# First attention: the product of probabilities and tokens in three fp32r passes instead of one fp32 pass

## The reference, cut to what matters

```python
kv = jnp.concatenate([memory, layer_input], axis=1)      # 64 + 64 = 128 tokens per sequence
q = (layer_input @ Wq).reshape(b, q_len, n_head, d_head) # 16 heads of 64
k = (kv @ Wk).reshape(b, kl, n_head, d_head)
v = (kv @ Wv).reshape(b, kl, n_head, d_head)
ac = jnp.einsum('bqhd,bkhd->bhqk', q + content_bias, k)
bd = rel_shift(jnp.einsum('bqhd,khd->bhqk', q + position_bias, r))
attn = jax.nn.softmax((ac + bd) / np.sqrt(d_head), axis=-1)  # masked before
ctx = jnp.einsum('bhqk,bkhd->bqhd', attn, v).reshape(b, q_len, n_head * d_head)
out = layer_norm(layer_input + ctx @ Wo, ln1_g, ln1_b)
```

## Time and profile before

| | us |
|---|---|
| median of 3 runs (1932.42, 1933.55, 5223.76) | 1933.55 |
| the profiled execution | 1940.73 |
| its span | 1939.2 |
| PE busy | 1621.0 (84%) |
| DVE busy | 1329.5 (69%) |
| ACT busy | 1199.0 (62%) |
| POOL busy | 946.9 (49%) |

### The profile page before, as it was taken

The page is one execution under the profiler, slowest core; times in us unless marked ns, Lnnn a source line. Parts: engine busy times, 40 slices in busy tenths (PEclk is TensorE's granted clock), DMA queues, the critical chain, the costliest instruction groups (busy, mean ns, idle before and its releaser), DMA issues. The chain is left out here.

```text
span 1939.2 us, 54781 instructions
## 1 busy us (share of the span) xinstructions
PE 1621.0 (84%) x17114; PEld 1295.5 (67%) x17114; DVE 1329.5 (69%) x4084; ACT 1199.0 (62%) x3451; POOL 946.9 (49%) x1389
## 2 busy tenths in 40 slices
PE   6999999999996869999999775479998884448981
PEld 5888888888884747667777662157776664437771
DVE  3777777777775638888777536668887883337772
ACT  2776777677674426677777335468888771137771
POOL 3354344444441454556665434534454444646773
PEclk8999999999998979999999787579999995559996
DMA  9676666766662022221000000000000000136765
GB/s 240 150 155 139 157 148 137 162 141 151 149 146 58 1 92 107 94 105 43 19 18 11 1 1 1 0 4 1 0 10 13 12 9 23 44 110 213 215 212 155
DMA packets 214819, 167.06 MB, mean 86 GB/s; under 512 B 27632, under 2 KB 188784, under 8 KB 214448
## 3 DMA queue, kind: packets, MB, share of 16 engines
q1 hardware_dynamic: 206128, 142.75, 29.1%
q0 software_dynamic: 8576, 22.88, 3.6%
HBM read 91.79 MB, written 73.76 MB: 85 GB/s over the span
## 5 line engine op out<-in xcount | busy, mean ns | idle before, releaser
L738 ACT ACTIVATE sb_probs<-sb_probs,sb_work 128x128 f32<-128x128 f32 x512 | 198.6, 406 | 120.3 <-DVE sb_work L641 120.3
L281 POOL TENSOR_SCALAR sb_next_var_eps<-sb_next_moments 128x1 f32<-128x1 f32 (+1 forms) x184 | 45.3, 246 | 433.2 <-DVE sb_next_moments L721 246.6
L890 POOL TENSOR_TENSOR sb_work<-sb_work,sb_cols 128x512 f32<-128x512 f32 x128 | 134.2, 1048 | 215.6 <-ACT sb_work L1107 133.6
L1033 DVE TENSOR_REDUCE sb_work<-PS 128x8 f32<-128x512 f32 x256 | 175.3, 685 | 46.9 <-PE PS L932 44.5
L1035 DVE TENSOR_TENSOR sb_work<-PS,sb_work 128x512 f32<-128x512 f32 x256 | 177.1, 692 | 8.8
L1067 ACT ACTIVATE sb_work<-sb_work 128x512 f32<-128x512 f32 x256 | 161.6, 631 | 33.4 <-DVE sb_work L1035 27.5
L906 PE MATMUL PS<-sb_ident,sb_work 128*128 128x128 f32 x1024 | 150.0, 287 | 15.9 <-ACT sb_work L1107 10.6
L959 PEld LDWEIGHTS PS<-sb_v_ones,sb_work 128*64 128x64 f32 x4096 | 133.0, 140 | 24.7 <-issue 16.9
L959 PE MATMUL PS<-sb_v_ones,sb_work 128*64 128x18 f32 x4096 | 144.9, 214 | 4.6 <-ACT sb_work L1073 2.8
L1073 ACT ACTIVATE sb_work<-PS 128x512 f32<-128x512 f32 x256 | 139.7, 594 | 10.1 <-PE PS L906 6.8
L906 PEld LDWEIGHTS PS<-sb_ident,sb_work 128*128 128x128 f32 x1024 | 113.8, 145 | 43.5 <-issue 31.3
(11 more groups left out here) (281 smaller groups left out, 4467.1 us busy)
## 6 DMA issues: line engine op xcount, KB each, us to landing
rel_scratch<-sb_work SPq DMA_DIRECT2D x64, 516.0 KB, 7.3
sb_work<-rel_scratch SPq DMA_DIRECT2D x64, 512.0 KB, 6.6
expert_rows<-sb_blank SPq DMA_DIRECT2D x36, 520.0 KB, 2.9
sb_w_up<-expert_halves SPq DMA_DIRECT2D x23, 512.0 KB, 3.6
sb_w_down<-expert_halves SPq DMA_DIRECT2D x23, 512.0 KB, 3.4
expert_halves<-sb_e_halves POOLq DMA_DIRECT2D x16, 512.0 KB, 6.2
sb_work<-expert_rows SPq DMA_DIRECT2D x23, 260.0 KB, 3.3
sb_e_raw<-e_W POOLq DMA_DIRECT2D x16, 256.0 KB, 5.3
```

Source lines behind the costliest of these rows:

```text
L738: ins = e.activation(probs[:, j], probs[:, j], ACT.Exp, bias=neg_max[:, j:j + 1], scale=-1.0, accum_out=row_sum[:, j:j + 1])
L890: e.tensor_tensor(k_masked[:, u3], k_sb[:, u3].rearrange("p (b k) -> p b k", b=2).unsqueeze(2) .to_broadcast([P, 2, 4, S]), col("place").u ...
L1033: e.tensor_reduce(top, mine, AX.X, ALU.max).then_inc(sem("att_max_ready"), 1)
```

## The change

The transposed probabilities are kept as two fp32r tensors, a rounded one and what is left, and the tokens likewise. The product becomes hi x hi + lo x hi + hi x lo, three passes that accumulate in the same bank. ScalarE writes the rounded probabilities out of PSUM, two instructions of 1024 columns ahead of its other work in a step. VectorE, where it copied, waits for that and subtracts. GpSimd makes kv_hi and kv_lo of the next tile, two instructions of 256 columns after the inverse deviations. Some tensors move and three semaphores are merged with others. The line numbers of the profile before do not hold in the new file: there the rounding is L764, the drain L773, the exponentials L757, the queries L785, the keys L795, and the helper of three passes L1223.

```diff
-        wvT, wo0 = probsT[0:DK], pkvT[0:DK]
+        wvT, wo0 = carve((H, P), H * KL)[0:DK], pkvT[0:DK]
...
+        rT = sb("rT", [P, H // 2, KL])
         kv_in = sb("kv_in", [P, 4, 2, D])
+        kv_hi, kv_lo = (sb("kv_" + part, [P, 2, 2, D], F32R) for part in ("hi", "lo"))
...
                     x_inv_std_pool(e, "l0", n + 1, n, 1)
+                if has(1):
+                    t, v = n + 1, (u + 1) % 2
+                    wait_alone(e, sem("l0_kv_loaded"), 48 * 4 if isinstance(t, int) and t < 4 else 48 * t + 48)
+                    wait_alone(e, sem("l0_pkv_done"), 4 * (t - 2) + 4)
+                    e.tensor_tensor(kv_hi[:, v], kv_in[:, (u + 1) % 4],
+                                    zeros[:, 0:1].unsqueeze(2).to_broadcast([P, 2, D]), ALU.add)\
+                        .then_inc(sem("l0_kv_split"), 1)
+                    wait_alone(e, sem("l0_kv_split"), 2 * t + 1)
+                    e.tensor_tensor(kv_lo[:, v], kv_in[:, (u + 1) % 4], kv_hi[:, v].bitcast(F32), ALU.subtract)\
+                        .then_inc(sem("l0_kv_split"), 1)
...
                         e.wait_ge(sem("l0_probsT_kept"), 2 * n + (1 if j == 0 else 2))
+                        if j == 0:
+                            e.wait_ge(sem("l0_kv_split"), 2 * n + 2)
                         if j == 3 and has(3):
                             e.wait_ge(sem("l0_kv_kept"), 2 * (n + 3) + 2)
-                        e.matmul(PS[:, (j + 1) % 4], kv_in[:, u, b], probsT[:, 8 * G:8 * G + 8, S * b:S * b + S],
-                                 start=True, stop=True).then_inc(sem("l0_pkv_done"), 1)
+                        heads, queries = slice(8 * G, 8 * G + 8), slice(S * b, S * b + S)
+                        product_in_parts(e, PS[:, (j + 1) % 4], (kv_hi[:, u % 2, b], kv_lo[:, u % 2, b]),
+                                         (probsT_hi[:, heads, queries], probsT_lo[:, heads, queries]))\
+                            .then_inc(sem("l0_pkv_done"), 1)
...
                 if has(0):
                     for half in range(2):
-                        e.wait_ge(sem("l0_probsT_done"), 4 * n + 2 * half + 2)
-                        e.tensor_copy(probsT[:, 8 * half:8 * half + 8].rearrange("p (g i) k -> p g (i k)", g=2),
-                                      PS[:, 2 * half:2 * half + 2]).then_inc(sem("l0_probsT_kept"), 1)
+                        e.wait_ge(sem("l0_probsT_rounded"), 2 * n + half + 1)
+                        r = slice(8 * half, 8 * half + 8)
+                        e.tensor_tensor(probsT_lo[:, r].rearrange("p (g i) k -> p g (i k)", g=2),
+                                        PS[:, 2 * half:2 * half + 2],
+                                        probsT_hi[:, r].bitcast(F32).rearrange("p (g i) k -> p g (i k)", g=2),
+                                        ALU.subtract).then_inc(sem("l0_probsT_kept"), 1)
...
+                if has(0):
+                    for half in range(2):
+                        e.wait_ge(sem("l0_probsT_done"), 4 * n + 2 * half + 2)
+                        e.activation(probsT_hi[:, 8 * half:8 * half + 8].rearrange("p (g i) k -> p g (i k)", g=2),
+                                     PS[:, 2 * half:2 * half + 2], ACT.Copy).then_inc(sem("l0_probsT_rounded"), 1)
                 if has(1):
                     exponentials(0)
```

More of the change, by code:

```diff
@@ L207, in build @@
         with ExitStack() as first:
-            VO, rel_bias, w_q0, w_k0_hi, w_k0_lo, rT, probs, probsT, pkvT = (
+            VO, rel_bias, w_q0, w_k0_hi, w_k0_lo, probs, probsT_hi, probsT_lo, pkvT = (
                 first.enter_context(nc.sbuf_tensor("sb_" + name, shape, dt))
@@ L211, in build @@
                                         ("w_q0", [P, H * DK], F32), ("w_k0_hi", [P, H * DK], F32R),
-                                        ("w_k0_lo", [P, H * DK], F32R), ("rT", [P, H // 2, KL], F32),
-                                        ("probs", [P, H, KL], F32), ("probsT", [P, H, P], F32),
+                                        ("w_k0_lo", [P, H * DK], F32R), ("probs", [P, H, KL], F32),
+                                        ("probsT_hi", [P, H, P], F32R), ("probsT_lo", [P, H, P], F32R),
                                         ("pkvT", [P, H, P], F32)))
@@ L470, in l0_tensor @@
                 ins.then_inc(sem("l0_table_done"), 1)
-            e.wait_ge(sem("l0_gap_wide"), 1)
+            e.wait_ge(sem("l0_gap_wide"), 2)
             for g in range(4):
@@ L611, in l0_vector @@
             e.wait_ge(sem("l0_rel_loaded"), 80)
-            e.tensor_tensor(bias_gap, position_bias[:, :], content_bias[:, :], ALU.subtract).then_inc(sem("l0_setup_kept"), 1)
-            e.wait_ge(sem("l0_setup_kept"), 1)
+            e.tensor_tensor(bias_gap, position_bias[:, :], content_bias[:, :], ALU.subtract).then_inc(sem("l0_gap_wide"), 1)
+            e.wait_ge(sem("l0_gap_wide"), 1)
             e.tensor_copy(gap_wide, bias_gap.unsqueeze(2).to_broadcast([P, H // 2, P])).then_inc(sem("l0_gap_wide"), 1)
@@ L626, in l0_vector @@
             e.wait_ge(sem("l0_qk_loaded"), 32)
-            e.tensor_copy(w_k0_hi[:, :], w_k0).then_inc(sem("l0_setup_kept"), 1)
-            e.wait_ge(sem("l0_setup_kept"), 2)
+            e.tensor_copy(w_k0_hi[:, :], w_k0).then_inc(sem("l0_gap_wide"), 1)
+            e.wait_ge(sem("l0_gap_wide"), 3)
             e.tensor_tensor(w_k0_lo[:, :], w_k0, w_k0_hi[:, :].bitcast(F32), ALU.subtract)\
-                .then_inc(sem("l0_setup_kept"), 1)
+                .then_inc(sem("l0_gap_wide"), 1)
             def step(k, u, has):
@@ L1382, in l2_vector @@
             e.memset(ones, 1.0).then_inc(sem("l2_ones"), 1)
-            e.tensor_scalar(half_bg, col("bg"), 0.5, None, ALU.mult).then_inc(sem("l2_half_bg"), 1)
+            e.tensor_scalar(half_bg, col("bg"), 0.5, None, ALU.mult).then_inc(sem("l2_ones"), 1)
             e.wait_ge(sem("l2_vis_kept"), 2)
@@ L1451, in l2_scalar @@
             e.activation(vis_gate, PS[:, 5, 128:128 + NB], ACT.Copy).then_inc(sem("l2_vis_kept"), 1)
-            e.wait_ge(sem("l2_half_bg"), 1)
+            e.wait_ge(sem("l2_ones"), 2)
             def step(k, u, head, front, back, late):
```

## The result

| | before | after |
|---|---|---|
| median of 6 runs each, us | 1933.67 | 1981.8 |
| profiled execution, us | 1940.73 | 1981.23 |
| its span, us | 1939.2 | 1979.7 |

The ratio is 1.025, with a 95% interval of 1.0233 to 1.0267. The forecast was 1955, with a range of 1925 to 1978. The two profiled executions differ by 40.5 us where 22 were forecast, so some 18 us are missing from the working. What follows accounts for the profiled ones.

The account below looks back on a forecast made before the run. Two loops were taken to share the bound: TensorE's own work (17.85 us a step) and one through x_lo (17.59). 29 x 0.62 + 2 + 2 = 22 us on the profiled 1940.73, less 0.4%, gave 1955, range 1925 to 1978.

Parts of the forecast that it names:

- Loop branches: ScalarE's loop pass begins every fourth step with an instruction on the path: seven times 0.3, 2 us.
- Rounding: ScalarE's copy of 1024 columns out of PSUM takes 0.99 us, so VectorE starts 1.05 us later; bounds 0.58 and 1.17.
- Subtraction: VectorE's subtraction in place of its copy of transposed probabilities takes the same 1.22 us, so nothing is added.
- x_lo and j = 3: x_lo, the tokens' low part, slips and TensorE's fourth product waits: +0.62 us a step, period 18.47.
- Product: On TensorE, twelve fp32r passes take 2.74 us a step instead of 3.43 for four fp32 products: 0.69 less.
- Splits: GpSimd's two instructions for kv_hi and kv_lo take about 0.65 to 0.75 us each, done before the product needs them.
- Tail: Steps 29 to 31 have no x_lo, so roundings sit bare in the chain: +2 us.
- Setup: Before the loop, loads only go to other places: nothing added.
- TensorE alone: Rival: only TensorE's own work counts, 29 x 0.69 = 20 us less, 1913; chance 0.10.
- Blocking of GpSimd and VectorE: Rival: subtractions and kv splits exclude each other, 1.3 us a step, 42 us more, 1976; chance 0.11.
- The clock: Rival: TensorE's idle time each step lowers its granted clock to 0.89, 40 us on top of 22, 1996; chance 0.05.
- Passes not as written: Rival: the product's passes are not what they seem, 1934; chance 0.02.

Follow-up runs that it names:

- e1_unrolled: Changed kernel with TensorE's steps of the first attention written out instead of looped, other engines keeping their loops: 1959.17 us, ratio 1.0112 to the kernel before.
- e3_shift128: Changed kernel with 128 already met waits on TensorE ahead of its loop, moving the loop's code but not its length: 1965.1 us, ratio 1.0147.
- e5_before_shift90: Kernel before with 90 already met waits on TensorE ahead of its unchanged loop: 1968.19 us, ratio 1.0154.
- e4_one_pass: Changed kernel with one pass, hi x hi, instead of three, and VectorE's rounding copy replacing ScalarE's rounding and the subtraction: 1914.68 us, ratio 0.989.
- e10_queries_first: As e9_swap_copies, with TensorE making the first half of the queries between products j = 2 and j = 3: 1920.62 us, ratio 0.9905.
- e6_swap: As e1_unrolled, with VectorE making the tokens of tile n + 3 before the scores of heads 4 to 7: 1948.58 us, ratio 1.0053.
- e7_swap_act: As e6_swap, with ScalarE making x_own and x_hi ahead of its exponentials: 1950.03 us, ratio 1.0058.
- e9_swap_copies: As e6_swap, with ScalarE draining products j = 0 and 1 ahead of its first exponentials: 1937.18 us, ratio 0.9995.
- e2_before_waits: Kernel before with nine already met waits on TensorE ahead of each product, giving its code the changed kernel's length: 1965.84 us, ratio 1.0156.
- e8_before_unrolled: Kernel before with TensorE's walk over the first layer's tiles written out instead of looped: 1937.8 us, ratio 1.0.

## Why the prediction was wrong

**The step that failed is "Loop branches".** It read: "Every fourth step ScalarE now begins its loop pass with an instruction on the path; VectorE lost 0.28 there where it had to wait [...] Seven times 0.3: 2 us." Measured were five back edges that cost 20.1 us. Two things were wrong. The number of branches back is five, not seven. And the price came from a wait of 0.28 that the trace before happened to show on VectorE, while the engine to ask about was TensorE, whose loop the change lengthens by nine instructions a step and moves. The kernel before has no such gap on TensorE, so no row of it gives a price; the sum put TensorE's own branch at nothing without a reason or a bound. ScalarE's branch, for which the 2 us stood, cost nothing that can be seen: in e1_unrolled, where ScalarE keeps its loop, the eight steps up to 208.74 and the 21 behind it are 18.53 us each. What the runs showed in its place: TensorE's code moved to where each branch back stops it for 3.1 us (e3_shift128, e5_before_shift90), with 45 packets of instructions more, and with the slow clock or a second stop behind it, 4.0 us for each of the five. Without that the forecast holds: e1_unrolled, the same kernel without TensorE's branch, took 1959.17 where 1955 was forecast, and 21.6 us more than the kernel before beside it where 22 were.

Point by point:

- *Rounding, 0.99 us from the slope of the earlier trace rows; VectorE 1.05 later.* Right: 1023 ns, VectorE waits 1.03. The bounds 0.58 and 1.17 were wide, the slope exact.
- *Subtraction, 1.22.* Right: two in 2.36, as the two copies had the earlier trace rows.
- *x_lo and j = 3, +0.62 a step, period 18.47.* Right: 18.47 in the step shown, 18.53 in e1_unrolled, 19.7 us in all instead of 18. e4_one_pass shows that this loop bounds the step. The step shown is one of the shorter ones.
- *Product, 0.69 less on TensorE.* The step of e10_queries_first, where nothing hides it, is 0.62 shorter. Its passes take 2.95 and not 2.74, since the two that come behind other matmuls hold the next back by 0.32 and not 0.23; 0.14 of these 0.21 comes back in the matmuls around them.
- *Splits of 0.65 and 0.75, hidden.* Right in the loop: 602 and 731 ns, done at 314.27. In the last tile kv_lo was late, which the prediction had not expected.
- *Tail, +2.* It was 0.6, although the last product waited for kv_lo.
- *Setup, nothing.* The profile after has 2.6 more ahead of tile 0, behind a load of the mask for which TensorE waited 5.9 us and before the change 2.6. In e1, e4, e6, e7, e9 and e10 tile 0 starts at 60.45 to 61.83, so the 2.6 aren't the change's; why it differs was not tried.

Timeline after, the product of the last tile, which waits for kv_lo:

```profile
652.67 0.76 PE L1223 MATMUL PS<-sb_probsT_hi,sb_kv_hi 128*128 128x512 f32 x1 [1.97 <-POOL sb_kv_lo L454]
```

The groups of the rounding and of the two splits after (busy us, mean ns of one, idle before):

```profile
L764 ACT ACTIVATE sb_probsT_hi<-PS 128x1024 fp32r<-128x1024 f32 x64 | 62.8, 1023 | 33.1 <-PE PS L511 33.1
L454 POOL TENSOR_TENSOR sb_kv_lo<-sb_kv_in,sb_kv_hi 128x256 fp32r<-128x256 f32 x31 | 22.7, 731 | 4.6
L450 POOL TENSOR_TENSOR sb_kv_hi<-sb_kv_in,sb_zeros 128x256 fp32r<-128x256 f32 x31 | 18.7, 602 | 0.0
```

*The rivals.* TensorE alone (1913): wrong by e4_one_pass; e10_queries_first shows what it would take. Blocking of GpSimd and VectorE (1976): its time is near the measured one, its mechanism is not there; the first subtraction and kv_hi start within 0.01 us of each other and both take their normal time. (The row on which this rival rests is read a little too high in the prediction: such a normalisation takes 1.22 where nothing blocks it, so 0.88 of the 2.10 was waiting and not 1.03.) The clock (1996): the idle time of 1.02 in each step did not lower it (1.00 in e1_unrolled over 440 us), but behind four of the five gaps, of about 3.1 us each, it fell to 0.50, which the rival had not in view. Passes not as written: twelve are there.

## What to carry to other kernels

Where an edit adds instructions to an engine that runs a hardware loop, or ahead of that loop, compare the packets of the instruction queue and look for "issue" gaps at the first instruction of each pass; where they appear, write the loop out or move it, and measure again. A wait that bounds a step in a loop is worth only the distance to the next one: e6_swap, e7_swap_act and e9_swap_copies each removed one and met another, and the gain of the three passes came only when the last was covered. Where a cost cannot be seen in the trace of before, bound it instead of setting it to nothing.

## What the runs showed of the hardware

- A branch back on TensorE cost nothing that can be seen (the kernel before, e3_shift128, e4_one_pass) or stopped it for 3.0 to 3.3 us (the kernel after, e5_before_shift90) or 2.4 to 2.8 (e2_before_waits), for the same loop by where its code lies. With what followed, a branch cost 3.95 us on the mean where the step had idle time, 4.6 and 5.5 where it had little or none. What in the position decides was not resolved: the waits tried were 36, 90 and 128.
- Behind ten of these fifteen stops the granted clock fell from 1.00 to 0.50 (from 2.4 to 1.2 GHz). Behind the other five it stayed at 1.00, and TensorE stopped a second time, for 0.3 to 1.5 us. The length of the first stop does not tell which: the clock fell behind one of 2.39 us (e2_before_waits) and stayed behind one of 3.15 (e5_before_shift90).
- Straight code is fetched without a visible cost: 91 packets in e1_unrolled and 90 in e8_before_unrolled against 59, and e8_before_unrolled takes as long as the kernel before. Written out, the five passes that the loop repeats are 32 packets more in e1_unrolled, 6.4 each, while a branch back that stops brings nine.
- ScalarE's copies out of PSUM take 280, 379, 581 and 1023 ns at 128, 256, 512 and 1024 columns: 0.8 to 0.9 ns for each further one. The type of the output hardly matters: at 512 columns another pair takes 598 ns (fp32) and 593 (fp32r) in e7_swap_act.
  Two of the four, from the groups of e7_swap_act (mean ns of one):

```profile
L767 ACT ACTIVATE sb_work<-PS 128x128 f32<-128x128 f32 x29 | 8.1, 280 | 34.9 <-PE PS L540 34.9
L769 ACT ACTIVATE sb_x_hi<-PS 128x256 fp32r<-128x256 f32 x29 | 11.0, 379 | 0.0
```

- GpSimd's fp32r instructions of 256 columns take 602 and 731 ns beside a VectorE subtraction with one operand in PSUM, and neither slows the other.
